# Head of a two-layer mixer in order of arrival, last group's chain in halves of tokens

## The reference

```python
# layer 0: 64 samples of x (32 channels x 512 positions)
att = softmax(gelu(gelu(c @ W0 + b0) @ W1 + b1) @ W2 + b2)        # 8 weights a sample
mix = einsum('boi,bih->boh', einsum('bk,koi->boi', att, weight), x) + (att @ bias_k)[:, :, None]
gates = softmax over the top 2 of (mix @ gate_w.T)                 # of 8 experts
x = x + mix @ base_w.T + base_b + 2 * sum_e gates_e * (mix @ A_e.T) @ B_e.T
# layer 1
h = grouped conv1d(x, kernel 9, pad 4) + (c @ c_weight.T) + bias
gates1 = softmax over the top 2 of (h @ router_w.T)                # of 4 experts
x = x + 4 * sum_e gates1_e * (h @ A1_e.T) @ B1_e.T
```

## Time and profile before

| what | us |
|---|---|
| median of the runs (lowest, highest) | 180.87 (180.74, 180.99) |
| the profiled execution, its own time | 182.46 |
| its span, first to last instruction | 180.7 |
| mean granted clock of TensorE | 0.991 of 2.4 GHz |
| busy: TensorE, VectorE, ScalarE, POOL | 173.0, 128.7, 82.0, 83.9 |
| lgw: issue starts at 1.24, to landing 3.4 | lands at 4.64 |
| ScalarE's first and second Gelu, start and length | 4.57 0.32, 5.41 0.31 |
| VectorE's last attention operation (att_d) | 7.76 to 8.10 |
| TensorE starts `turn_lw(1)` | 52.94 |

### The profile page before, as it was taken

How to read it: one execution, slowest core, us unless ns; L and a number is a source line. 1 busy time by engine, 2 the same in 40 slices (tenths; PEclk the granted TensorE clock), 3 DMA queues, 4 the chain that set the end, 5 groups by cost and what they waited for, 6 DMA issues and landing times.

```text
span 180.7 us, 3138 instructions
## 1 busy us (share of the span) xinstructions
PE 173.0 (96%) x1125; PEld 161.7 (89%) x1125; DVE 128.7 (71%) x271; ACT 82.0 (45%) x189; POOL 83.9 (46%) x86
## 2 busy tenths in 40 slices
PE   7889999999999999999999999999999999999980
PEld 6778888988998799999989999999899999999870
DVE  1359899968966944797998334987998953368671
ACT  3767656942633546634225176443224464235020
POOL 8023605992065779952007379830006786065000
PEclk9979999999999999999999999999999999999999
DMA  6999100003300240000023000000041000000336
GB/s 174 268 389 387 41 2 0 0 4 123 111 0 4 87 145 2 0 4 0 0 90 147 0 0 4 0 0 0 4 174 58 2 5 0 0 0 0 120 116 232
DMA packets 6495, 12.16 MB, mean 67 GB/s; under 512 B 720, under 2 KB 1360, under 8 KB 6480
## 3 DMA queue, kind: packets, MB, share of 16 engines
q1 hardware_dynamic: 6048, 11.44, 18.1%
q10 hardware_dynamic: 432, 0.52, 0.9%
...
## 4 chain that ended last, share of the span: by engine, by line
PE 86%; DVE 5%; DMA 4%; issue 1%; SPq 1%; DVEq 0%
PE ps L963 21%; PE ps L965 21%; PE ps L964 21%; PE ps L1055 7%; DMA xT_s<-in_xT_dram 4%; PE ps L977 3%; PE ps L994 2%; PE ps L1148 1%; PE ps L1149 1%; PE ps L1037 1%; PE ps L1235 1%; PE ps L1066 1%; DVE xsl L675 1%; DVE xT_s L724 1%; DVE x1T L730 1%
## 5 line engine op out<-in xcount | busy, mean ns | idle before, releaser
L963 PE MATMUL ps<-xw_h,xTh 128*128 128x264 f32 (+1 forms) x96 | 30.4, 317 | 0.0
L964 PE MATMUL ps<-xw_l,xTh 128*128 128x264 f32 (+1 forms) x96 | 29.9, 312 | 0.0
L965 PE MATMUL ps<-xw_h,xTl 128*128 128x264 f32 (+1 forms) x96 | 29.8, 310 | 0.0
L336 POOL TENSOR_TENSOR xTl<-xT_s,xTh 128x512 fp32r<-128x512 f32 x12 | 15.2, 1300 | 24.7 <-ACT xTh L426 16.9
L341 POOL TENSOR_TENSOR zl<-outb,zh 128x340 fp32r<-128x340 f32 x15 | 14.4, 963 | 14.7 <-ACT zh L461 7.8
L352 POOL TENSOR_TENSOR x1Tl<-x1T,x1Th 128x512 fp32r<-128x512 f32 x12 | 16.0, 1346 | 9.4 <-DVE lw L703 9.4
L743 DVE TENSOR_TENSOR outb<-ps,s_sb 128x340 f32<-128x340 f32 x16 | 8.2, 512 | 16.8 <-PE ps L965 12.5
L1055 PEld LDWEIGHTS ps<-mixT,xp 128*128 128x128 f32 x128 | 16.4, 191 | 2.3 <-DVE x1T L730 1.1
L964 PEld LDWEIGHTS ps<-xw_l,xTh 128*128 128x128 f32 x96 | 18.1, 188 | 0.1
L963 PEld LDWEIGHTS ps<-xw_h,xTh 128*128 128x128 f32 x96 | 18.1, 188 | 0.1
L965 PEld LDWEIGHTS ps<-xw_h,xTl 128*128 128x128 f32 x96 | 18.1, 188 | 0.0
...
## 6 DMA issues: line engine op xcount, KB each, us to landing
...
```

What stands on the lines that cost most here:

```text
L336: nc.gpsimd.tensor_tensor(lo[:, c, :], xT_s[:, g % 2, c, :], hi[:, c, :].bitcast(F32), ALU.subtract).then_inc(x_lo, 1)
L963: nc.tensor.matmul(dst, sh, mh, start=start and c == 0, stop=False)
L964: nc.tensor.matmul(dst, sh, ml, start=False, stop=False)
L965: last = nc.tensor.matmul(dst, sl, mh, start=False, stop=stop and c == n - 1)
```

## The change

**Head.** x and base_w of group 0 are loaded chunk by chunk in turn, then x of group 1, lb, a second copy of base_w with its columns on the partitions (`wrow`, new, 4 x 256 KB, into outb), az, side; tapw and b1T follow behind `wsum_ok`, since they use the same memory. `sum_w` is made by ScalarE: four copies of wrow that also accumulate. TensorE takes `x_logits` by chunk, and `x_base` of chunk 0 stands ahead of `x_logits` of chunks 1 to 3; the sums of lgw and az over chunks are made by POOL (`lgw_t`, `az_t`), so that one matmul each is left of four. The context matmul moves behind `make_y(0)`, its bias to ScalarE. `bias_row(1)` moves ahead of `x_base(1,2)`.

**POOL.** It makes the mixing weights of group 3: one product of 1024 elements a partition and three adds of 512, 256 and 128 (the middle one is left out below). Its order in the head is new: two lows of x, two more behind the first `lw_ok`, the mixing weights, ue, ud, `az_t`, the low parts of sw, uw, vw, `bias_rows(1)`, the four `x1_low`, tap, b1.

**Tail.** The outputs 2 and 3 of group 2 get their x1 on TensorE (`with_x1`) and are copied by ScalarE. `mw` of group 3 is weighed in two halves and split into high and low before it is turned (`mw_hl`); each half of 256 tokens is turned, copied once (one half by ScalarE, one by VectorE) and multiplied. Outputs 0 and 1 are copied and stored in halves, 2 and 3 whole, from the memory of x1.

```diff
     for c in range(DC):
         load_xT(0, c)
-    sp.dma_start(side_s[:, :], side).then_inc(in_side, 16)
+        sp.dma_start(wT_s[:, c, :], wT[:, c, :]).then_inc(in_base[c], 16)
     for c in range(DC):
-        sp.dma_start(wT_s[:, c, :], wT[:, c, :]).then_inc(in_base[c], 16)
...
+        load_xT(1, c)
     sp.dma_start(lbT_s, lbT).then_inc(in_lb, 16)
...
+        sp.dma_start(wrow_s[:, c, :], wrow[:, c, :]).then_inc(in_wrow[c], 16)
+    sp.dma_start(az_s, az).then_inc(in_az, 16)
+    sp.dma_start(side_s[:, :], side).then_inc(in_side, 16)
+    sp.wait_ge(wsum_ok, DC)
     sp.dma_start(tapw_s, tapw).then_inc(in_tap, 16)
     sp.dma_start(b1T_s, b1T).then_inc(in_b1, 16)
...
+    pool.wait_ge(base_lo, DC)
+    x_low(1, 0)
+    x_low(1, 1)
+    pool.wait_ge(lw_ok, 1)
+    x_low(1, 2)
+    x_low(1, 3)
...
+    pool.wait_ge(attl_ok, 1)
+    pool.wait_ge(in_wrep, 16)
+    nc.gpsimd.tensor_tensor(prod_last, att_last[:, :, :].unsqueeze(2).to_broadcast([P, TG, C, K0]),
+                            wrep_s[:, :, :].unsqueeze(1).to_broadcast([P, TG, C, K0]), ALU.mult).then_inc(tree_ok, 1)
+    pool.wait_ge(tree_ok, 1)
+    nc.gpsimd.tensor_tensor(prod_last[:, :, :, 0:4], prod_last[:, :, :, 0:4], prod_last[:, :, :, 4:8],
+                            ALU.add).then_inc(tree_ok, 1)
...
+    nc.gpsimd.tensor_tensor(agg[:, TG * (G - 1):TT, :], prod_last[:, :, :, 0], prod_last[:, :, :, 1],
+                            ALU.add).then_inc(aggl_ok, 1)
...
-    pool.wait_ge(lb_lo, 1)
-    for c in range(DC):
-        x_low(1, c)
...
     bias_rows(1)
+    pool.wait_ge(lw_ok, 2)
+    for t in range(TG):
+        x1_low(0, t)
     pool.wait_ge(tap_hi, 1)
     nc.gpsimd.tensor_tensor(tap_l[:, :, :].rearrange("p k c -> p (k c)"), tapw_s,
...
-    pool.wait_ge(lw_ok, 2)
-    for t in range(TG):
-        x1_low(0, t)
...
+    act.wait_ge(in_lgw, 16)
+    nc.scalar.activation(xw_h[:, :, 0:LG], lgw_s[:, :, :], ACT.Copy).then_inc(lgw_hi, 1)
...
+    x_high(1, 1)
     act.wait_ge(lgsum_mm, 1)
     nc.scalar.activation(lg_sum[:, :], ps[:, LGS, 0:LG], ACT.Copy).then_inc(lgsum_ok, 1)
-    base_high(1)
-    xl_out(0)
-    base_high(2)
-    base_high(3)
...
-    nc.scalar.activation(uw_h[:, :, :], ue[:, :, :], ACT.Copy).then_inc(suv_hi, 1)
+    x_high(1, 2)
+    x_high(1, 3)
+    gate_exp(0, gate0, dif0_ok, ex0_ok)
...
     lwT_high(0)
-    act.wait_ge(in_tap, 16)
...
+    for c in range(DC):
+        act.wait_ge(in_wrow[c], 16)
+        nc.scalar.activation(wrow_s[:, c, :], wrow_s[:, c, :], ACT.Copy,
+                             accum_out=sum_w[:, c:c + 1]).then_inc(wsum_ok, 1)
+    act.wait_ge(in_az, 16)
+    nc.scalar.activation(sw_h[:, :, :], az_s[:, 1, :, :], ACT.Copy).then_inc(suv_hi, 1)
+    mix_place(1)
+    act.wait_ge(dif_ok, 1)
+    nc.scalar.activation(uw_h[:, :, :], ue[:, :, :], ACT.Copy).then_inc(suv_hi, 1)
+    act.wait_ge(dif_ok, 2)
+    nc.scalar.activation(vw_h[:, :, :], ud[:, :, :], ACT.Copy).then_inc(suv_hi, 1)
+    for g in range(2, G):
         mix_place(g)
     for t in range(TG):
         xa_out(1, t)
     bias_high(1)
     act.wait_ge(pjsum_mm, 1)
...
+    act.wait_ge(in_side, 16)
+    for j in range(BT):
+        rows = slice(j * C, (j + 1) * C)
+        last = nc.scalar.activation(ctxbias[rows, :], ctx_b[rows, j:NB:BT], ACT.Identity,
+                                    bias=side_s[rows, S_FS:S_FS + 1])
+    last.then_inc(ctx_ok, 1)
+    act.wait_ge(in_tap, 16)
+    nc.scalar.activation(tap_h[:, :, :].rearrange("p k c -> p (k c)"), tapw_s, ACT.Copy).then_inc(tap_hi, 1)
+    act.wait_ge(in_b1, 16)
+    nc.scalar.activation(b1_h[:, :], b1T_s, ACT.Copy).then_inc(b1_hi, 1)
...
+    sums_high(0, 0)
+    sums_high(0, 1)
     p0_out(1, 2)
...
-    for t in range(TG):
-        sums_high(0, t)
+    sums_high(0, 2)
+    sums_high(0, 3)
...
+    for c in range(DC // 2, DC):
+        act.wait_ge(d_mm, DC * (p - 1) + c + 1)
+        act.wait_ge(out_done[c], 16 * (p - 1))
+        nc.scalar.activation(outb[:, c, :], ps[:, DLT[c], :], ACT.Copy).then_inc(out_act, 1)
+    for h in range(2):
+        act.wait_ge(mwa_ok, h + 1)
+        nc.scalar.activation(mw_hl[:, 2 * h:2 * h + 2, 0, :], mw[:, 2 * h:2 * h + 2, :], ACT.Copy).then_inc(mwa_hi, 1)
+    act.wait_ge(turn_mm, 1)
+    nc.scalar.activation(mwT[:, 0:HALF], ps[:, TURN[0], 0:HALF], ACT.Copy).then_inc(turn_act, 1)
...
+        if p == G - 1:
+            for h in range(2):
+                weigh_mid(2 * h, 2 * h + 2).then_inc(mwa_ok, 1)
+        else:
+            weigh_mid(0, TG).then_inc(mw_ok, 1)
...
+    dve.wait_ge(lgw_hi, 1)
+    minus(xw_l[:, :, 0:LG], lgw_s[:, :, :], xw_h[:, :, 0:LG]).then_inc(lgw_lo, 1)
...
-    base_low(1)
+    nc.vector.tensor_copy(att_last[:, :, :], attb[:, TG * (G - 1):TT, :]).then_inc(attl_ok, 1)
+    x_low(2)
...
     route0(0)
     bias_low(0)
+    dve.wait_ge(base_lo, DC)
+    mix_sum(2, prods[1], TG, TG)
     dve.wait_ge(lb_hi, 1)
     minus(lb_l[:, :], lbT_s, lb_h[:, :]).then_inc(lb_lo, 1)
-    dve.wait_ge(base_lo, DC)
-    mix_sum(2, prods[1], TG, TG)
-    dve.wait_ge(wsum_mm, 1)
-    nc.vector.tensor_copy(sum_w[:, :], ps[:, WSUM, 0:DC]).then_inc(wsum_ok, 1)
+    lwT_low(0)
     mix_half(2, 0)
-    lwT_low(0)
     mix_half(2, 1)
-    mix_half(3, 0)
-    mix_half(3, 1)
-    dve.wait_ge(suv_lo, 3)
+    dve.wait_ge(in_side, 16)
     for c in range(DC):
         bias_x(0, c)
+        if c == DC // 2:
+            dve.wait_ge(aggl_ok, 1)
         make_x1(0, c)
-    dve.wait_ge(agg_ok, MIX_STEPS[G - 1])
...
     route0(1)
     sums(0, 0)
     sums(0, 1)
+    bias_x(1, 0)
     lwT_low(1)
-    bias_x(1, 0)
     sums_low(0, 0)
     sums(0, 2)
+    bias_x(1, 1)
     sums_low(0, 1)
     sums(0, 3)
     make_x1(1, 0)
     sums_low(0, 2)
     sums_low(0, 3)
-    for c in range(1, DC):
-        bias_x(1, c)
-        make_x1(1, c)
+    make_x1(1, 1)
+    bias_x(1, 2)
+    make_x1(1, 2)
+    bias_x(1, 3)
+    make_x1(1, 3)
...
-    make_out(p - 1, 2)
-    make_out(p - 1, 3)
-    mwT_low(p)
...
+    for h in range(2):
+        dve.wait_ge(mwa_hi, h + 1)
+        minus(mw_hl[:, 2 * h:2 * h + 2, 1, :], mw[:, 2 * h:2 * h + 2, :], mw_hl[:, 2 * h:2 * h + 2, 0, :]).then_inc(mwa_lo, 1)
...
+        if with_x1:
+            for n, part in enumerate(x1_parts(p)):
+                nc.tensor.matmul(ps[:, DLT[c], :], ident_r[:, :], part[:, c, :], start=n == 0, stop=False)
...
-    keep_busy(4, 4)
+    keep_busy(4, 2)
...
     nc.tensor.matmul(attb_b, place_r[:, :, :].rearrange("b j c -> b (j c)"),
                      att_d[:, :, :].rearrange("b t k -> b (t k)"), start=True, stop=True).then_inc(attb_mm, 1)
-    x_logits(0, (1,))
-    x_logits(1)
+    keep_busy(4, 3)
+    for t in range(TG):
+        x_base(0, t, (0,))
     pe.wait_ge(attT_ok, 1)
     nc.tensor.matmul(mixb_b, early_s[0:K0, A_MB:A_MB + P], attT[:, :], start=True, stop=True).then_inc(mixb_mm, 1)
-    pe.wait_ge(in_side, 16)
...
-    for t in range(TG):
-        x_base(0, t, (0,))
+    for c in range(1, DC):
+        x_logits(c)
     for t in range(TG):
         x_base(0, t, (1,))
+    pe.wait_ge(xl_ok, 2)
+    pe.wait_ge(lgt_ok, 1)
+    nc.tensor.matmul(ps[:, LGS, 0:LG], ones[:, :], lgw_t[:, 2, :], start=True, stop=True).then_inc(lgsum_mm, 1)
...
-    pe.wait_ge(base_lo, DC)
-    for n, part in enumerate((base_h, base_l)):
-        for c in range(DC):
-            last = nc.tensor.matmul(ps[:, BSUM, :], ones_r[:, :], part[:, c, :],
-                                    start=n + c == 0, stop=n == 1 and c == DC - 1)
-    last.then_inc(bsum_mm, 1)
     for c in range(2, DC):
         for t in range(TG):
             x_base(0, t, (c,))
-    pe.wait_ge(bsum_ok, 1)
-    for c in range(DC):
...
-    for c in range(DC):
+    for chunks in ((0, 1), (2, 3)):
         for t in range(TG):
-            x_first(1, t, (c,))
+            x_first(1, t, chunks)
...
-    pe.wait_ge(in_az, 16)
+    pe.wait_ge(azt_ok, 1)
+    pe.wait_ge(in_side, 16)
     pe.wait_ge(x1_ok, DC)
-    for m in range(2):
-        for h in range(2):
...
+    nc.tensor.matmul(ctx_b, side_s[:, S_CTX:S_CTX + P], early_s[:, A_COND:A_COND + NB],
+                     start=True, stop=True).then_inc(ctx_mm, 1)
+    nc.tensor.matmul(psum_b, ones[:, :], az_t[:, 2, :], start=True, stop=True).then_inc(pjsum_mm, 1)
     x_base(1, 0)
     x_base(1, 1)
+    bias_row(1)
     x_base(1, 2)
     turn_lw(1)
     x_base(1, 3)
-    bias_row(1)
...
-    experts1(p, 2)
-    experts1(p, 3)
-    for n in range(4):
-        place_x1(n)
-    keep_busy(6, 4)
-    turn_mw(i)
-    keep_busy(6, 8)
-    place_x1(4)
-    for n in range(len(DLT_LAST)):
-        add_experts(n)
+    pe.wait_ge(ident_ok, 1)
+    experts1(p, 2, True)
+    experts1(p, 3, True)
+    pe.wait_ge(ze_ok, TG * G)
+    pe.wait_ge(zo_ok, TG * G)
+    for c in (2, 3, 0, 1):
+        place_x1(0, c)
+    place_x1(1, 0)
+    turn_last(0)
+    turn_last(1)
+    place_x1(1, 1)
+    pe.wait_ge(turn_act, 1)
+    for c in (2, 3, 0, 1):
+        add_experts(0, c)
+    pe.wait_ge(turn_dve, 1)
+    for c in (2, 3, 0, 1):
```

(1 more changed line is left out.)

262 lines of the change are left out of this document (139 added, 123 removed).

## The result

The kernel after takes 1.0167 of the kernel before (95% interval 1.013 to 1.0205): 184.0 us against 180.9, or 3.0 us more, where the prediction had 181.1 and no change. (Ratios here leave out executions of either kernel that another disturbance made longer; the plain median of all six is 184.7.) The profiled execution took 184.99 us by its own time, 183.3 by its span, at a mean granted clock of 0.977; before it was 182.46, 180.7 and 0.991.

What follows compares the result with a forecast made beforehand. TensorE's queue plus both ends was taken as the bound, with POOL the new long leg. Head -0.3, clock +1.1 and tail -0.6 gave +0.2 on 182.46, 182.7; less 1.59, 181.1 us, no tellable change; range 177.0 to 183.3.

Steps and rivals of the forecast that it cites:

- POOL's leg: POOL in the head, from the first lw to the end of `bias_rows(1)`: 16.8 plus 0.8 for VectorE's turns, ending 41.7.
- ScalarE's: ScalarE behind `bias_rows(1)`, from `bias_high(1)` to the exponent: ends at 47.3, so the second lw comes at 48.9.
- VectorE in turns with POOL: First group's sums and lows: one VectorE operation passes at each end of a POOL one, so `make_x1(1,0)` ends at 59.8.
- the 1.59 taken off at the end: Last step of the sum: the runs' median is 1.59 below the profiled execution, so 182.7 became 181.1.
- `mix_logits(0)` done at 19.5: TensorE's head: less work there ends `x_first(1)` at 31.5 instead of 37.71, hence `mix_logits(0)` at 19.5.
- the slower rival: Low clock in the head again, at 10.8 under dense `x_base`: costs 1.7, arriving as +1.9, 182.8; chance 0.25.
- The clock behind the wait: After TensorE's 4.2 us pause in `make_y(1)`, part of a 1.2 GHz stretch falls on work: +1.1, two thirds of 1.7.
- B: Stretch from the start of the second lw to the first `z_full` on VectorE: measured 18.45, 14.87 before.
- The tail: Last group's chain: first expert matmul at 173.5 instead of 174.24, stores earlier; gain 0.4 to 0.9, taken as -0.6.
- A: Stretch from the start of the first lw to the second on VectorE: measured 24.96, 23.70 before.
- The faster one: POOL's leg or VectorE's turns are shorter; tap_l and b1_l out of the way gives -3.75, 177.1; chance 0.33.
- My bound for a slow case: Upper end of the range, 183.3: the slower rival's price with a second low clock stretch.

Runs made afterwards that it cites:

- the best kernel: Kernel after, last group's mixing weights back on VectorE, tap_h and b1_h ahead of xa copies, tap_l and b1_l directly behind `bias_rows(1)`; 178.38 us, ratio 0.9863.
- more fillers: Kernel after, with 32 filler matmuls ahead of `make_y(1)`'s third chunk and 4, 4, 6 instead of 2, 2, 2 in the head; 182.58 us, ratio 1.0117.
- the fillers: Kernel after, with 32 filler matmuls on TensorE ahead of the third chunk of `make_y(1)`; 182.94 us, ratio 1.0112.
- its own run: Kernel before, with only the edits of the last group's chain (the new tail); 180.05 us, ratio 0.9952.

## Why the prediction was wrong

**The mechanism was right, the sum was not.** POOL's leg, then ScalarE's, then VectorE in turns with POOL, then TensorE idle, then the low clock: each was predicted and each is in the profile. `bias_rows(1)` ended at 43.23 (predicted 41.7), `make_x1(1,0)` at 61.27 (59.8), the wait is 4.31 (4.2).

**The step that failed most on the medians: the 1.59 taken off at the end.** The prediction worked out 182.7 for an execution and took 1.59 off, the distance of the profile before from its median. But 1.28 of the 1.59 lie in that profile's slow head: with the same head and a granted clock of 1.00 the first `z_full` came at 64.06 instead of 65.34. The times of the forecast, from the first lw at 24.1 on, were worked out for a head at full clock (`x_logits` at 2.9 instead of 4.62). They held no slow head that could be taken off again.

**The term that failed most in the profile: `mix_logits(0)` done at 19.5, and with it the first lw at 24.1.** It was ready at 25.63, 1.5 late. In the kernel with `bias_rows(1)` early and in the best kernel `x_base` starts at 9.81 and 9.46 (predicted 9.4) and the first lw is ready at 24.67 and 24.47; in the profile after it starts at 10.60. So the step was right for an execution in which TensorE is quick at the start. In the profile after it is not: eight passes of `x_logits` took 1.81 us at half clock (1.17 in the best kernel). This is the slower rival's mechanism, which had 0.25; the clock fell at 7.7 instead of 10.8. It isn't what made the kernel slower than forecast, though: two executions of the kernel after with a mean clock of 0.991, which is one low stretch of 3.4 us and not two (an estimate), still took 183.67 and 183.85. The first lw started between 23.8 and 26.4 in the profiled executions with this head, by how long TensorE was at its lower speed at the start (last section). What decides that stays open: more fillers didn't.

**From the first lw to the second:** 24.8 predicted, 24.96 measured; right, also where it counted the new mixing weights (4.7 for 5.3). What I had not seen is that shortening this leg alone brings only 0.4 to 1.5, as ScalarE's is nearly as long and VectorE has to do what POOL gives up.

**The clock behind the wait:** +1.1 predicted, 1.5 by the fillers.

**From the second lw on:** together with the clock, B should have been 66.1 - 48.2 = 17.9 and was 18.45. The turns of VectorE came as forecast: `sums_low(0,1)` and `sums(0,3)` passed one at each end of a POOL operation.

**The tail:** -0.6 predicted, -0.46 in the profile, -0.9 (0.3 to 1.4) by its own run.

**The account.** In the profile, 1.5 for the first lw, 0.15 for A, 0.5 for B and 0.15 for the tail are the 2.3 between 182.7 and 184.99. On the medians the gap is 2.9, and its parts are others. From the start of the first `z_full` to the end of the execution it takes 116.64 us in the kernel after, and 116.5 to 117.0 in ten other kernels with this tail in which nothing comes back behind it (116.5 to 116.6 in seven of them). So an execution of 184.0 has its first `z_full` at 67.4 and, with A and B as measured, its first lw ready at 24.7; this is an estimate, and the kernel with tap_l and b1_l later, whose head is the same, has 24.64. Then 0.6 of the gap is the first lw, 0.15 A, 0.5 B, 0.15 the tail, and the 1.5 that is left is the 1.59.

**The rivals.** The faster one said that with tap_l and b1_l out of the way the gain would be 3.75. The best kernel gives two thirds of that (2.5), but only with the mixing weights moved too: with the two operations moved alone the time is 1.005, and moved later it is 1.036. I priced their absence and not the place where they would have to go. My bound for a slow case, a second low stretch in addition, gave 183.3; the measured 184.0 lies above. This bound stood on 180.87 too, with the 1.59 taken off; without that it would have been 184.9.
